# Two-layer transformer block: q/k of the first 20 heads through two banks and ahead of the scores, with weight folds, result, memsets, scales and rows of q placed elsewhere

## What is computed

```python
xn = layernorm(x)
q, k, v = (xn @ w + b for w, b in ...)              # 8 x 256 x (16 heads x 128)
weights = softmax(q @ k.T / sqrt(128) - 1e10 * (1 - mask))
x = x + (weights @ v) @ w_o + b_o + ffn_fp8(xn)
xn = layernorm(x)
x = x + attention16(xn)                             # 16 heads of 16
h = fwht(xn * SU_ug) / 64
up, gate = h @ W_up.T * (scale_u * 64), h @ W_gate.T * (scale_g * 64)
x = x + fwht(silu(gate) * up * SU_dp) / 64 @ W_down.T * (scale_d * 64)
```

## Time and profile before

| what | value |
|---|---|
| median of 3 runs | 893.56 us (890.87 to 896.01) |
| the profiled execution: its own time | 894.07 us |
| its span in the profile | 891.5 us |
| busy over the span: PE, DVE, ACT, POOL | 90%, 79%, 77%, 55% |
| mean granted TensorE clock | 0.968 of full speed |

### The profile page before, as it was taken

One profiled execution on the slowest core, in us unless ns is written; L12 is line 12 of the kernel. 1 busy time (PEld: TensorE's weight loads), 2 busy tenths in 40 slices (PEclk: granted clock), 3 DMA queues, 4 the chain that ended last, 5 costly groups with the idle time before them and its releaser, 6 DMA issues.

```text
span 891.5 us, 21313 instructions
## 1 busy us (share of the span) xinstructions
PE 803.1 (90%) x7136; PEld 627.8 (70%) x7136; DVE 700.3 (79%) x2011; ACT 687.5 (77%) x1997; POOL 486.6 (55%) x753
## 2 busy tenths in 40 slices
PE   3777888899999999999999999999999999976985
PEld 1334566667788877888788878887887788854753
DVE  6987786667888787878787878788878887886673
ACT  4797796646798898889888988788888888886563
POOL 4701455543466565656665666566656565676463
PEclk9998898999999999999999999999999999999987
DMA  9332577213474567556646765566556655756454
GB/s 294 135 117 89 141 179 173 48 28 61 89 114 72 115 129 108 86 111 126 116 79 101 139 112 81 107 127 111 90 105 127 113 93 95 126 108 124 64 107 83
DMA packets 284012, 98.62 MB, mean 111 GB/s; under 512 B 241920, under 2 KB 279552, under 8 KB 283520
## 3 DMA queue, kind: packets, MB, share of 16 engines
q1 hardware_dynamic: 283904, 97.27, 56.0%
HBM read 30.11 MB, written 8.39 MB: 43 GB/s over the span
## 4 chain that ended last, share of the span: by engine, by line
PE 59%; DVE 14%; ACT 7%; DMA 6%; issue 3%; POOL 3%; SPq 2%; POOLq 0%; ACTq 0%; DVEq 0%
PE ps L790 35%; PE ps L873 8%; DMA arena<-arena 5%; PE ps L981 4%; DVE arena L784 3%; PE ps L964 3%; ACT arena L1060 2%; DVE arena L1205 2%; DVE arena L783 2%; PE ps L992 2%; PE ps L834 2%; PE ps L886 2%; ACT arena L779 2%; PE ps L966 2%; ACT arena L778 1%
## 5 line engine op out<-in xcount | busy, mean ns | idle before, releaser
L784 DVE SCALAR_TENSOR_TENSOR arena<-ps,bqk,arena 128x256 bf16<-128x256 f32 x416 | 187.2, 479 | 41.0 <-ACT arena L779 39.9
L790 PE MATMUL ps<-arena,wqkv 128*128 128x256 bf16 x1728 | 216.7, 276 | 0.0
L779 ACT ACTIVATE arena<-ps,bqk 128x256 bf16<-128x256 f32 x416 | 177.8, 465 | 24.7 <-PE ps L790 17.4
L790 PEld LDWEIGHTS ps<-arena,wqkv 128*128 128x128 bf16 x1728 | 171.5, 99 | 23.4
L1410 POOL TENSOR_SCALAR arena<-arena,rc 128x128 f32<-128x128 f32 (+1 forms) x256 | 106.3, 428 | 141.6 <-DVE rc L1228 141.6
L1060 ACT ACTIVATE arena<-arena,nb 128x128 f32<-128x128 f32 (+1 forms) x256 | 114.3, 447 | 84.2 <-DVE nb L1205 83.3
L1401 POOL TENSOR_TENSOR arena<-arena 128x512 bf16<-128x512 f32 x115 | 136.0, 1184 | 64.9 <-ACT arena L778 64.8
L778 ACT ACTIVATE arena<-arena 128x384 bf16<-128x384 f32 (+1 forms) x256 | 139.4, 577 | 13.8 <-DMA arena<-arena 7.6
L1417 POOL TENSOR_SCALAR arena<-arena,rc 128x256 f32<-128x256 f32 x256 | 120.2, 483 | 52.7 <-DVE rc L1232 52.4
L1060 ACT ACTIVATE arena<-ps,nb 128x256 f32<-128x256 f32 x256 | 118.3, 471 | 17.6 <-DVE nb L1212 16.1
L873 PE MATMUL ps<-wo,arena 128*128 128x256 bf16 x768 | 106.3, 275 | 20.0 <-DVE arena L784 19.4
(11 more groups left out here) (113 smaller groups left out, 1228.6 us busy)
## 6 DMA issues: line engine op xcount, KB each, us to landing
arena<-arena SPq DMA_TRANSPOSE x256, 3.1
scratch_qk<-arena SPq DMA_DIRECT2D x28, 128.0 KB, 1.9
arena<-scratch_qk SPq DMA_DIRECT2D x84, 32.0 KB, 1.9
arena<-scratch_qk SPq DMA_DIRECT2D x42, 64.0 KB, 2.9
arena<-in_x SPq DMA_DIRECT2D x4, 512.0 KB, 9.5
arena<-in_w_gating SPq DMA_DIRECT2D x4, 512.0 KB, 8.4
arena<-in_w_q SPq DMA_DIRECT2D x4, 512.0 KB, 4.9
arena<-in_w_k SPq DMA_DIRECT2D x4, 512.0 KB, 5.9
```

The source lines that it names most:

```text
L779: return nc.scalar.activation(out, in_, ACT.Identity, bias=bias)
L784: return nc.vector.scalar_tensor_tensor(out=out, in0=in_, scalar=bias, in1=hi, op0=ALU.add, op1=ALU.subtract)
L790: last = nc.tensor.matmul(out, lhsT, rhs, start=(n == 0), stop=(n == len(steps) - 1))
```

## The change

1. **q/k projection.** For slots below 20 (`TWO`), P stands ahead of S in PE's list, and heads of odd number go to bank `BK_M` instead of `BK_QK`. `BK_M` is used by layer 1 later; its first user waits for `qk0_lo` of 20. From slot 20 on P is where it was.
2. **Fold on DVE.** `fold(s)` is no longer first in DVE's slot: it stands behind `qk0_low(s)`. PE's F and D stay last in PE's slot, with their waits.
3. **Result.** `result(b)` stands behind `rec_1`, ahead of `hidden`, where it was behind everything else of the slot but the splits.
4. **Memsets.** They write 32-bit words instead of bf16 (half the elements). `qs` is cleared in two halves, in slots 17 and 19 instead of 18, behind POOL's fold, which now also comes before the memset of `ks`.
5. **Scales.** `scu` is loaded in four pieces of 256 KB in slots 8 to 11, the down scales in slot 12; each DVE fold waits for its own piece.
6. **Rows of q.** The six DMA issues of `stack_q(b, 1)` stand behind `turn0` and `turn1` of their slot instead of ahead of them.

```diff
+        def bank_qk0(n):
+            return BK_M if n < TWO and n % 2 else BK_QK
...
+                if s < TWO:
+                    proj_qk0(s)
                 if 0 <= s - 1 < NG0:
                     scores0(s - 1)
...
-                if s < NG0:
+                if TWO <= s < NG0:
                     proj_qk0(s)
...
             for s in range(SLOTS):
                 last = s >= NG0
-                fold(s)
...
                 if s < NG0:
                     qk0_low(s)
+                fold(s)
...
                 for n in heads_in[s]:
                     rec_1(n)
+                for b in y_in[s]:
+                    result(b)
...
-                if s in seconds_of_q:
-                    stack_q(seconds_of_q[s], 1)
                 if 0 <= s - 2 < NG0:
                     turn0(s - 2)
                 for n in heads_in[s - 1]:
                     turn1(n)
+                if s in seconds_of_q:
+                    stack_q(seconds_of_q[s], 1)
...
+                if 8 <= s < 12:
+                    n = slice(512 * (s - 8), 512 * (s - 7))
+                    sp.dma_start(scu[:, n], t["sc_u"][n].partition_broadcast(P)).then_inc(scale_loaded[s - 8], 16)
```

More of the change, by code:

```diff
@@ L189, in build @@
                      ("wo1", 0): 10}
+        scale_loaded = [sem(f"scale_loaded{i}") for i in range(4)]
         stage_loaded = [sem(f"stage_loaded{i}") for i in range(STG)]
@@ L762, in free_m @@
             last = before_m.get((kind, n))
-            if last is not None:
+            if last is None:
+                pe.wait_ge(qk0_lo, TWO)
+            else:
                 pe.wait_ge((exp1, x1T_lo, qkv1_lo, o1_lo)[last[0]], last[1] + 1)
@@ L847, in proj_qk0 @@
                 for w in range(2):
-                    last = group(ps[:, BK_QK, w * T:(w + 1) * T],
+                    last = group(ps[:, bank_qk0(n), w * T:(w + 1) * T],
                                  [(wqkv0[:, a, w, k, g * HD0:(g + 1) * HD0], cur[:, b % 2, c, k, :])
@@ L1097, in qk0_high @@
                 for w in range(2):
-                    last = high(qk0[:, 0, n % 2, w, :], ps[:, BK_QK, w * T:(w + 1) * T], bqk0[:, w, g:g + 1])
+                    last = high(qk0[:, 0, n % 2, w, :], ps[:, bank_qk0(n), w * T:(w + 1) * T], bqk0[:, w, g:g + 1])
                 last.then_inc(qk0_hi, 1)
@@ L1237, in qk0_low @@
                 for w in range(2):
-                    last = low(qk0[:, 1, n % 2, w, :], ps[:, BK_QK, w * T:(w + 1) * T], qk0[:, 0, n % 2, w, :],
+                    last = low(qk0[:, 1, n % 2, w, :], ps[:, bank_qk0(n), w * T:(w + 1) * T], qk0[:, 0, n % 2, w, :],
                                bqk0[:, w, g:g + 1])
@@ L1322, in fold @@
                     j, m = divmod(u, KD)
-                    if u == 0:
-                        dve.wait_ge(scales_loaded, 32)
+                    if m == 0:
+                        dve.wait_ge(scale_loaded[j], 16)
                     upto(dve, fold_lo, u - 2)
@@ L1332, in fold @@
                     dve.wait_ge(down_fold_ps, m + 1)
+                    if m == 0:
+                        dve.wait_ge(scales_loaded, 16)
                     nc.vector.scalar_tensor_tensor(out=staged_dn[:, m, :], in0=ps[:, BK_Y, 0:D],
@@ L1390, in dve_program @@
                         normalise(b)
-                for b in y_in[s]:
-                    result(b)
                 for c in splits_in[s]:
@@ L1457, in pool_program @@
                     pool_butterfly(pool)
+                fold(s)
                 if s == 14:
                     weights_ready(pool, ("l1", 0))
-                    nc.gpsimd.memset(ks[:, :, :, :], 0.0).then_inc(ks_zero, 1)
-                if s == 18:
+                    nc.gpsimd.memset(ks[:, :, :, :].rearrange("p b h t -> p (b h t)").bitcast(F32), 0.0).then_inc(ks_zero, 1)
+                if s in (17, 19):
                     weights_ready(pool, ("wo1", 0))
-                    nc.gpsimd.memset(qs[:, :, :, :], 0.0).then_inc(qs_zero, 1)
-                fold(s)
+                    n = slice(4 * (s == 19), 4 * (s == 19) + 4)
+                    nc.gpsimd.memset(qs[:, n, :, :].rearrange("p h e t -> p (h e t)").bitcast(F32), 0.0).then_inc(qs_zero, 1)
         def sp_program(sp):
@@ L1513, in stack_q @@
                 if b == 0:
-                    sp.wait_ge(qs_zero, 1)
+                    sp.wait_ge(qs_zero, j + 1)
                 sp.wait_ge(spilled[0][b % 2], 32 * (b // 2 + 1))
@@ L1565, in sp_program @@
                     sp_later_y(sp, PAIRS - 1)
-                if s == 10:
-                    sp.wait_ge(xT_stored, 32 * (PAIRS - 1))
                 if g == 10 and b < B:
                     load_y(b)
-                if s == 10:
-                    sp.dma_start(scu, t["sc_u"].partition_broadcast(P)).then_inc(scales_loaded, 16)
+                if s == 8:
+                    sp.wait_ge(d0_ps, PAIRS)
+                    sp.wait_ge(xT_stored, 32 * (PAIRS - 1))
+                if 8 <= s < 12:
+                    n = slice(512 * (s - 8), 512 * (s - 7))
+                    sp.dma_start(scu[:, n], t["sc_u"][n].partition_broadcast(P)).then_inc(scale_loaded[s - 8], 16)
+                if s == 12:
                     sp.dma_start(sc_d, t["sc_d"].partition_broadcast(P)).then_inc(scales_loaded, 16)
```

1 line of the change is left out of this document (added).

## The result

| | before | changed |
|---|---|---|
| median (lowest to highest) | 893.77 us (890.87 to 896.01, 4 runs) | 903.44 us (900.28 to 904.37, 4 runs) |
| ratio, 95% interval | | 1.0102 (1.0073 to 1.0131) |
| profiled execution, its span | 894.07, 891.5 us | 900.28, 898.5 us |
| mean granted clock in that span | 0.968 | 0.970 |
| T5, from the span's start | 108.09 us | 107.45 us |

The forecast was 899.5 (890.5 to 906).

A forecast was written before the change was run, and what follows sets the result against it. PE sets the slot time, so its idle time or added work before slot 20 shifts everything after. 7.65 + 1.4 + 0 - 3.8 - 1.6 + 2 = +5.65 on 894.07 gave 899.7; the median forecast was 899.5, range 890.5 to 906.

The forecast's parts named there:

- The two waits: Slots 13 to 19: PE waits 1.3 us at O, and 0.5 to 1.8 us at F for DVE's fold.
- Slots 13 to 19: Slots with folds: 51.6 us against 43.95 before, +7.65; slots 15 to 18 take 7.81 each.
- the clock: Slots 13 to 19: one or two more slow slots at the lower clock, +2 us, from 0 to +7.
- Slots 20 to 22: D still waits for DVE's fold there: 16.8 us against 15.36 before, +1.4.
- Slots 5 to 12: Slots without folds, P uncovered but the transpose wait gone: 42.8 us against 42.31, taken as 0, from -3 to +2.
- Slots 2 to 4: Early slots, where PE was early at S and P is covered: end some 0.5 us earlier.
- Rows of q: Steady part: six of `attend1`'s seven waits for transposes go, -3.8 us, or 0 if the delay only moves on.
- Result: Steady part: the result fills DVE's idle time before `hidden` and O's 0.74 us wait halves, -1.6; at best -3.3.
- Memsets: POOL's memsets are off the path once the fold has moved: cost 0; half the elements may halve their time.
- The second bank pays: Rival, chance 0.22: slots 2 to 12 win 3 us, the steady part 3.8 + 3.3, no further clock fall; about 892.5.
- Faster: Rival, chance 0.10: PE's wait for `fold_f` is hidden, slots 13 to 19 take 42.8 us; about 887.
- The clock in every slot: Rival, chance 0.13: the clock falls in every slot with a fold, +5 us on the forecast, 904.5.

The follow-up runs named there:

- e_fold_first: The changed kernel with DVE's fold first in its slot again; 891.17 us, ratio 0.9953 to the kernel before.
- e_rest: The changed kernel with P behind S in every slot, one bank, and DVE's fold first again; 882.25 us, ratio 0.9858 to the kernel before.
- e_scales_only: The kernel before with only the scales loaded in four pieces in slots 8 to 11; 893.27 us, ratio 0.9983.
- e_memset_only: The kernel before with only the memset part: 32-bit words, `qs` in two halves, POOL's fold ahead; 892.41 us, ratio 0.9965.
- e_banks_only: The changed kernel with P behind S and DVE's fold first, second bank for odd heads kept; 881.02 us, ratio 0.9863 to the kernel before.
- e_p_behind: The changed kernel with P behind S in every slot and one bank; 888.02 us, ratio 0.9923 to the kernel before.
- e_fold_mid: The changed kernel with P behind S, one bank, and DVE's fold between `o0_low` and `p0_low`; 879.43 us, ratio 0.9822 to the kernel before.
- e_stack_only: The kernel before with only the six DMA issues of `stack_q(b, 1)` moved behind the transposes; 891.2 us, ratio 0.9965.
- e_result_only: The kernel before with only `result(b)` moved ahead of `hidden`; 892.6 us, ratio 0.9974.
- e_p_only: The kernel before with only P ahead of S and the second bank below slot 20; 902.06 us, ratio 1.008.
- e_fold_only: The kernel before with only DVE's fold moved behind `qk0_low`; 896.45 us, ratio 1.001.

## Why the prediction was right, and where its sizes were off

**What set the time.** Right: PE's own order. The two waits are where the prediction put them, and each move undone alone gives back about what was expected of it (15.4 us for 15, 12.3 for 14). The waits are a little shorter than said: O's 1.14 us instead of 1.3, and F's in the even slots 0.30, below the 0.5 named as its least.

**Slots 13 to 19.** The sum said 51.6 us at a full clock and 2 for the clock. Measured 55.74: slots 15, 16 and 18 took 7.76, 7.77 and 7.76 us against 7.81 foretold, slot 14 took 6.89 against 6.93. Slots 13, 17 and 19 took 8.39, 9.22 and 7.95, which is 1.5, 1.4 and 1.5 over, and there F lasts 1.89 us instead of 1.04 and what follows is slow as well. The step that was mis-sized is the clock: +4.1 where +2 was taken, three slots and not one or two, inside its own bound of +7. The 2 was counted as slow slots "more than now", but the 51.6 holds none at all, so those that the kernel before had belong in the term too.

**When the clock fell.** Behind equal waits of 1.14 and 1.59 us the clock fell to its lower level, 1.2 GHz, in slots 13 and 17 and not in 15; it fell in 19 behind 0.92 and 1.59 us, and in no even slot (1.14 and 0.3). Two windows of the changed kernel, behind the F of slot 15 and at that of slot 19 (the granted clock is the third column from the end):

```profile
170.00:172.00 2.00, 1.19 (x7) 0.70 (x8) 2.00 (x3) 1.52 (x4) 1.69 (x2) 1.00 0.75 170
...
204.00:206.00 2.00, 2.00 (x8) 1.05 (x7) 1.01 (x3) 0.00 (x0) 0.12 (x1) 0.50 0.00 0
```

The Trainium skill, "TensorE: Matmul & The Clock Gate", section "HAM oscillation — how this bites in real kernels", describes a loop in which PE waits longer for data than it computes, and lets the clock fall in every round there. No run here shows such a loop: PE's two waits in slot 15 come to 2.7 of 7.76 us, and the clock fell in three of the seven rounds.

**Slots 20 to 22.** 16.87 measured, 16.8 foretold. F's wait is gone there, D has it (0.47 and 1.33 us) in slots 20 and 21. Slot 22 took 5.56 us, as before, and its D does not wait; that the sum still fits is in part luck.

**Slots 5 to 12.** 44.07 measured, 42.8 foretold. Slots 5 to 7 were 16.71 (16.7 foretold) and slot 12 6.50 (6.42). Slots 8 to 11 were 20.86, not 19.64. These rows show the step that failed: the prediction let T follow S by 0.70 in every slot, but in slot 9 DVE came late, and in slot 11 A waited for a transpose.

```profile
133.34 0.66 PE L799 MATMUL ps<-arena 128*128 128x128 bf16 x6
134.36 0.29 DVE L1216 CUSTOM_DVE_ANT_0 arena<-ps,mask 128x128 f32<-128x128 f32 x1
...
142.51 0.50 PE L973 MATMUL ps<-arena 128*128 128x256 bf16 x3 [0.67 <-DMA arena<-arena]
```

This understates the miss, though. The forecast called the sum of P ahead and of the scales 0 here; the runs show a loss of 4.9 us (`e_fold_first` 44.47, `e_rest` 39.56) and a gain of 2.7 (`e_scales_only` 39.61). Two terms of 3 to 5 us hid in a 0; their sum was off by 1.8.

**Slots 2 to 4.** T5 came 0.64 us earlier, 0.5 foretold: slot 2 won 2.0 (7.20 to 5.22), slot 4 lost 1.05 (7.06 to 8.11), and T1 came 0.28 later. The wait of S of 4.81 us, which the prediction names, stayed 4.82; that of the first S fell from 1.71 to 0.40, since a P now stands ahead of it. With one P more done by then, V stands directly behind the next S. The first row is before, the second the changed kernel:

```profile
91.64 2.62 PE L790 MATMUL ps<-wqkv,arena 128*128 128x512 bf16 x6
```

```profile
89.36 2.77 PE L799 MATMUL ps<-wqkv,arena 128*128 128x512 bf16 x6
```

DVE splits this V (at 94.93 us before, 93.11 after) ahead of the `max_0` that ends the slot.

**Rows of q and result.** -5.4 foretold, -7.4 measured from T23 on. Rows of q: -3.8 said, 3.8 less in the profile of its own run. Result: -1.6 said, 3.2 less in the profile of its own run. The mis-sized term is the result: of O's wait of 0.74 the prediction gave back 0.4, and 0.47 to 0.5 came back at each of the five places, in the changed kernel too; and the 0.4 of loss in the last stage did not show, for from the first O of that stage that waits (800.88 us before, 807.95 after) to the end it is 90.6 us in both. That makes 2.4 where 1.6 was said. The further 0.8 of its own run, and 1.2 of the 7.4, are spread over waits too small for me to assign. One of the five rows of the changed kernel:

```profile
448.73 0.83 PE L882 MATMUL ps<-wo,arena 128*128 128x256 bf16 x6 [0.27 <-DVE arena L793]
```

**Memsets.** In the changed kernel no fold of DVE in slots 13 to 19 waits for POOL, which fits the 0; no run undoes part 4 there. But `e_memset_only` shows that part 4 is worth 2.5 us in slot 18 where DVE's fold stands first. The Trainium skill, "VectorE: DVE Perf Modes", section "Zero memsets can be issued as uint32 (trn2)", says for VectorE that a memset's time goes by elements whatever their size; on POOL the rows above agree (0.88 and 0.86 ns for an element).

**The sum.** By terms: slots 13 to 19 +11.8 (said +7.65 and +2), 20 to 22 +1.5 (+1.4), 5 to 12 +1.8 (0), to T5 -0.6 (-0.5, taken as 0), steady part -7.4 (-5.4): +7.0 of span, where +5.65 was said. The clock came out 2 dearer, slots 5 to 12 nearly 2 dearer, the result nearly 2 better. The profiled execution's own time rose by 6.2, since 1.8 us lie around its span and not 2.57. At 900.28 it is 0.8 us over the forecast's 899.5, and the median another 3.2 higher, with clocks of 0.965 to 0.967 in the three other executions. The forecast had gone the other way here: it took the median 0.5 below the profiled execution.

**The rivals.** *The second bank pays* is refuted by `e_banks_only` and `e_p_behind`. *Faster* is refuted by F's waits. The rule on banks that the prediction sets beside it does not bear on it: the change gives another bank to q and k, and F keeps its one. *The clock in every slot* did not come, and its price was too low: at the 1.4 to 1.5 us that a slow slot cost, seven come to 10 (an estimate), not 7. One more slip is in the chances: three quarters of 0.55 and 0.13 make 0.54 for slower than 898.0, not 0.58.

## What to carry to other kernels

A second buffer was worth nothing where the consumer that frees the first was already waited for by the instruction ahead; and moving a block ahead of a wait pays only if the engine idles at that wait (the first S) and not if the block was covering another wait (O's, in most slots from 4 on). Ask of each block that is moved what it stands in front of now and what it no longer stands in front of. Where two engines hand work to and fro in a loop, put each step directly behind the last thing that somebody waits for sooner (`e_fold_mid`): both "first" and "behind everything" put waits on PE in slots 15 to 19 here, the place between them none. And a change of six parts may hold -12 us and +22 us at once; with two of them undone it is faster than either kernel.

## What the runs showed of the hardware

- The clock fell in other slots from kernel to kernel at the same waits. In nine kernels O waits 2.23 or 2.24 us for DVE ahead of V in slot 16. V lasts 1.46 us behind it in four of them (before, `e_rest`, `e_banks_only`, `e_scales_only`) and 2.10 to 2.61 us in five (`e_memset_only`, `e_stack_only`, `e_result_only`, `e_p_only`, `e_fold_first`). The rows of `e_memset_only`:

```profile
172.99 0.83 PE L873 MATMUL ps<-wo,arena 128*128 128x256 bf16 x6 [2.24 <-DVE arena L784]
...
173.66 2.25 PE L790 MATMUL ps<-wqkv,arena 128*128 128x512 bf16 x6
```

- The wait of slot 12 behind the one load of 1 MB was 1.03, 1.48, 1.96, 2.13 and 3.28 us in five kernels that issue it the same way (`e_result_only`, `e_stack_only`, before, `e_fold_only`, `e_memset_only`), and 0.38 in a sixth, `e_p_only`, where P stands ahead. A single profile prices such a wait only to within 2 to 3 us, so slots 12 to 16 of one profile each are weak evidence on a part that doesn't touch them. All profiles together are better evidence for part 5: with P behind S, slots 5 to 12 took 40.7 to 44.3 us in the five kernels with the one load and 39.4 to 39.6 in the five with four pieces.
- PE's wait for the last transpose came in two sizes, and the move of `stack_q` does not tell them apart: 3.49 to 3.57 us in `e_stack_only`, the changed kernel and `e_banks_only`, and 3.48 in `e_memset_only`, which has no such move; 2.77 to 3.00 us in the ten others, five of them with the move. So the 0.6 us by which it grew in `e_stack_only` are not shown to be a cost of the move. What sets the size is open.
